# Routed experts: another order on GpSimd, down weights fetched once per expert, a copy added on ScalarE

## What is computed

```python
x = x + xattn(layernorm(x), ctx)                      # 16 sequences of 128 rows x 512
xt = layernorm(x).reshape(2048, 512)                  # 2048 tokens, h = 512
probs = softmax(xt @ Wr.T + bias)                     # 16 experts
w, idx = top_k(probs, 2); w = w / (w.sum() + 1e-9)
g, u = xt @ Wg[e], xt @ Wu[e]                         # 512 -> 256 each, expert e
y[e] = (silu(g) * u) @ Wd[e]                          # 256 -> 512
out = x + sum over the two chosen e of w * y[e] + shared expert(xt)
```

## Time and profile before

| | us |
|---|---|
| Median of 3 runs | 844.56 (840.42 to 849.78) |
| The profiled execution | 844.39 |
| Its span, first to last instruction | 842.6 |
| Mean granted PE clock, as a share of full speed | 0.917 |

### The profile page before, as it was taken

One profiled execution on the slowest core, in us unless ns is written; L12 is line 12 of the kernel. 1 busy time (PEld: TensorE's weight loads), 2 busy tenths in 40 slices (PEclk: granted clock), 3 DMA queues, 4 the chain that ended last, 5 costly groups with the idle time before them and its releaser, 6 DMA issues.

```text
span 842.6 us, 14106 instructions
## 1 busy us (share of the span) xinstructions
PE 689.8 (82%) x4136; PEld 334.9 (40%) x4136; DVE 400.5 (48%) x1426; ACT 315.2 (37%) x630; POOL 434.2 (52%) x640
## 2 busy tenths in 40 slices
PE   3378889999889888887699898959979887888791
PEld 1134445555555555433344444323323332333230
DVE  3387778888888887622425743212221222122210
ACT  3136556666666665552121122212222222222220
POOL 2466677777777777572000002246655454565542
PEclk9568899999999999898699999988998999999986
DMA  9967566566666664116777253567877777778772
GB/s 334 148 78 87 92 91 104 105 109 116 113 110 109 107 109 75 29 31 249 298 244 247 86 176 112 158 187 180 240 218 203 200 203 207 206 182 227 206 197 36
DMA packets 73684, 130.78 MB, mean 155 GB/s; under 512 B 18064, under 2 KB 42768, under 8 KB 71440
## 3 DMA queue, kind: packets, MB, share of 16 engines
q1 hardware_dynamic: 59264, 100.31, 47.7%
q0 software_dynamic: 9600, 20.98, 12.6%
q10 hardware_dynamic: 4752, 8.65, 3.1%
HBM read 84.55 MB, written 19.14 MB: 123 GB/s over the span
## 4 chain that ended last, share of the span: by engine, by line
DMA 31%; PE 28%; issue 13%; POOL 13%; DVE 5%; SPq 4%; ACT 3%; POOLq 2%; DVEq 0%; ACTq 0%
DMA out<-y_out,scatter_i 11%; DMA out<-y_out,scatter 10%; DMA wgu<-wgu 6%; PE bank L717 6%; POOL wgu L448 3%; POOL wgu L446 3%; PE bank L748 3%; PE bank L730 3%; SPq L322 3%; PE bank L556 3%; PE bank L572 2%; DMA rows<-xn_rows,gather_i 2%; PE bank L598 2%; PE bank L586 2%; POOL wgu L455 2%
## 5 line engine op out<-in xcount | busy, mean ns | idle before, releaser
L1081 DVE CUSTOM_DVE_ANT_0 bank<-bank,cb 128x192 f32<-128x192 f32 (+1 forms) x512 | 187.2, 415 | 60.4 <-PE bank L556 57.6
L730 PE MATMUL bank<-wgu,rowsT 128*64 x320 | 156.2, 634 | 2.7 <-DVE X L1308 2.3
L732 PE MATMUL bank<-X,rowsT 128*64 128x512 f32 x320 | 156.2, 634 | 0.0
L1294 DVE TENSOR_TENSOR act_in<-act_in,bank 128x256 f32<-128x256 f32 x56 | 23.6, 421 | 267.2 <-ACT act_in L979 259.1
L892 ACT ACTIVATE wgu<-bank 128x384 f32<-128x384 f32 (+1 forms) x256 | 125.2, 544 | 64.7 <-PE bank L572 64.1
L556 PE MATMUL bank<-wgu 96*128 96x192 bf16 (+1 forms) x512 | 97.4, 277 | 25.6 <-DMA wgu<-wgu 15.4
L495 POOL DMA_INDIRECT rows<-xn_rows,gather_i x40 | 47.7, 1193 | 125.9 <-issue 109.6
L446 POOL TENSOR_SCALAR_AFFINE_SELECT wgu<-wgu 128x512 f32<-128x512 f32 (+1 forms) x128 | 74.5, 582 | 71.1 <-ACT wgu L892 70.8
L509 POOL DMA_INDIRECT out<-y_out,scatter_i x40 | 60.3, 1508 | 84.1 <-DMA out<-y_out,scatter 43.5
L572 PE MATMUL bank<-wgu 99*128 99x192 bf16 (+1 forms) x512 | 73.7, 265 | 18.2 <-DMA wgu<-wgu 12.1
L509 POOL DMA_INDIRECT out<-y_out,scatter x40 | 58.3, 1456 | 52.6 <-DMA out<-y_out,scatter_i 30.0
(11 more groups left out here) (154 smaller groups left out, 938.0 us busy)
## 6 DMA issues: line engine op xcount, KB each, us to landing
X<-w_d SPq DMA_DIRECT2D x80, 512.0 KB
wgu<-wgu SPq DMA_DIRECT2D x192, 128.0 KB, 4.7
wgu<-w_gu SPq DMA_DIRECT2D x16, 1024.0 KB, 6.9
out<-y_out ACTq DMA_DIRECT2D x17, 256.0 KB, 6.0
wgu<-ctx SPq DMA_DIRECT2D x16, 256.0 KB, 4.5
xn_rows<-xn SPq DMA_DIRECT2D x16, 256.0 KB, 3.1
rows<-xn_rows ACTq DMA_DIRECT2D x16, 256.0 KB, 2.7
X<-x SPq DMA_DIRECT2D x1, 3072.0 KB, 16.0
```

Source lines behind the costliest of these rows:

```text
L730: mm(gb[k.buf][0:GROUP, :], rowsT[:, k.buf, c, 0:GROUP], wgu[:, bass.ds(e * 2048 + 512 * c, 512)], start=(c == 0), stop=(c == 3))
L732: last = mm(gb[k.buf][GROUP:P, :], rowsT[:, k.buf, c, GROUP:P], gu_half[:, k.buf, 512 * c:512 * c + 512], start=(c == 0), stop=(c == 3))
L1081: last = v.tensor_tensor_reduce(o, o, cb[:, B_MASK + off:B_MASK + off + w], 1.0, MASKED * 2.0, ALU.add, ALU.max, rowmaxes[n % 2][:, h + i, ...
```

## The change

It does five things in the routed stage.

1. **Adds.** `added` now counts by parity of the block, 32 for each block. Add (j, 0) waits for `result(j)` and, only if its expert is new, until both adds of block j-1 have landed. Add (j, 1) waits until both adds of block j-1 have landed, and for (j, 0) if its expert is new. Rows without a token are left out by the bounds check (`TOKENS - 1`, no error) and no longer written to the spare rows. The empty last slot now takes expert 15, as the other empty slots do, and slot 72 no longer counts as a new expert.
2. **Gathers.** `rows` has three buffers. POOL's order is gather(j+5), add_group(j, 0), add_group(j, 1).
3. **Down weights.** SP loads each expert's down weights once, 16 loads, into a ring of three in X (WD_RING), each when the last block of the expert three before is done (`last_i`), and one at a time.
4. **A copy on ACT.** Slot 0 reads the ring in place, at an address from a register. For slot 1, `wd_copy(k)`, last in ACT's step, reads two registers from tables, waits for down(k-1) and for the weights, and copies 128x1024 float32 inside X. `routed_down(k)` on PE waits for that copy.
5. **Tables.** `routing_blocks` also builds `place_i` (which ring buffer), `need_i` and `last_i`, and `order_i` in another form.

```diff
@@ load_wd is replaced, SP @@
+            for e in range(EXPERTS):
+                if e >= WD_RING:
+                    done = sp.value_load(last_i[0:1, e - WD_RING:e - WD_RING + 1], min_val=SEQS, max_val=SEQS + BLOCKS)
+                    stand(sp, SP, dn_mm, done)
+                sp.dma_start(wd[:, e % WD_RING * 1024:(e % WD_RING + 1) * 1024], w_d[e]).then_inc(wd_in, 16)
+                sp.wait_ge(wd_in, 16 * (e + 1))
@@ gather @@
-                n = SEQS + j
-                after(pool, t_mm, n - 1)
+                if j < 2:
+                    pool.wait_ge(t_mm, SEQS - 1 + j)
+                elif j > 2:
+                    pool.wait_ge(t_mm, SEQS + j - 2)
@@ add_group @@
-                if j > 0:
-                    pool.wait_ge(added[g], 16 * j)
-                if j > 0 or g > 0:
-                    stand(pool, POOL, added[1 - g], seen)
-                pool.wait_ge(y_ready, n + 1)
+                if g == 0:
+                    pool.wait_ge(y_ready, SEQS + j + 1)
+                    if j > 0:
+                        stand(pool, POOL, added[(j - 1) % 2], seen)
+                else:
+                    if j > 0:
+                        pool.wait_ge(added[(j - 1) % 2], 32 * ((j + 1) // 2))
+                    stand(pool, POOL, added[j % 2], seen)
...
-                    y_out[GROUP * g:GROUP * g + GROUP, n % 2, :], None, bounds_check=TOKENS + P - 1,
-                    oob_is_err=True, compute_op=ALU.add).then_inc(added[g], 16)
+                    y_out[GROUP * g:GROUP * g + GROUP, j % 2, :], None, bounds_check=TOKENS - 1,
+                    oob_is_err=False, compute_op=ALU.add).then_inc(added[j % 2], 16)
@@ POOL's loop @@
             for j in range(BLOCKS):
+                if j + AHEAD < BLOCKS:
+                    gather(j + AHEAD)
                 add_group(j, 0)
                 add_group(j, 1)
-                if j + AHEAD < BLOCKS:
-                    gather(j + AHEAD)
@@ PE @@
+            def wd_place(k):
+                return pe.value_load(place_i[0:1, (k.n - SEQS) * SUB:(k.n - SEQS) * SUB + 1], min_val=0,
+                                     max_val=WD_RING - 1)
...
-            def routed_down(k):
-                pe.wait_ge(wd_in[k.buf], 16 * SUB * (k.round - SEQS // 2 + 1))
+            def routed_down(k, place):
+                pe.wait_ge(wd_copied, k.n - SEQS + 1)
                 pe.wait_ge(at_ready, k.n + 1)
                 pe.wait_ge(y_ready, k.n - 1)
                 for c in range(2):
...
+                    mm(yb[k.buf][0:GROUP, :], actT[:, k.buf, c, 0:GROUP], wd[:, bass.ds(place * 1024 + 512 * c, 512)],
+                       start=(c == 0), stop=(c == 1))
+                    last = mm(yb[k.buf][GROUP:P, :], actT[:, k.buf, c, GROUP:P], wd_half[:, c, :],
+                              start=(c == 0), stop=(c == 1))
@@ result, ACT @@
-                    for g in range(2):
-                        act.wait_ge(added[g], 16 * (j - 1))
+                    act.wait_ge(added[j % 2], 32 * (j // 2))
@@ the end of ACT's step @@
                 if k.n + 2 < SEQS + BLOCKS:
                     rows_copy(k.plus(2))
+                wd_copy(k)
+
+            def wd_copy(k):
+                j = k.n - SEQS
+                place = act.value_load(place_i[0:1, j * SUB + 1:j * SUB + 2], min_val=0, max_val=WD_RING - 1)
+                need = act.value_load(need_i[0:1, j * SUB + 1:j * SUB + 2], min_val=16, max_val=16 * EXPERTS)
+                if j == 0:
+                    act.wait_ge(y_ready, SEQS // 2)
+                else:
+                    act.wait_ge(dn_mm, k.n)
+                stand(act, SCALAR, wd_in, need)
+                nc.scalar.copy(wd_half.rearrange("p a n -> p (a n)"),
+                               wd[:, bass.ds(place * 1024, 1024)]).then_inc(wd_copied, 1)
```

More of the change, by code:

```diff
@@ L49 @@
 RING = 4
+WD_RING = 3
 FIRST_UNIT, LAST_UNIT = -25, UNITS * (SEQS - 1) + 40
@@ L227, in xattn_moe_kernel @@
         rows_in = [sem(f"rows_in{i}") for i in range(2)]
-        wd_in = [sem(f"wd_in{i}") for i in range(2)]
+        wd_in, wd_copied = sem("wd_in"), sem("wd_copied")
         y_stored = [sem(f"y_stored{i}") for i in range(2)]
-        gathered = [sem(f"gathered{i}") for i in range(2)]
+        gathered = [sem(f"gathered{i}") for i in range(3)]
         added = [sem(f"added{i}") for i in range(2)]
@@ L704, in turn_rows @@
                 if shared:
-                    pe.wait_ge(rows_in[k.buf], 16 * (k.round + 1))
-                else:
-                    pe.wait_ge(gathered[k.buf], 16 * (k.round - SEQS // 2 + 1))
+                    held = k.buf
+                    pe.wait_ge(rows_in[held], 16 * (k.round + 1))
+                else:
+                    held = (k.n - SEQS) % 3
+                    pe.wait_ge(gathered[held], 16 * ((k.n - SEQS) // 3 + 1))
                 after(pe, t_ready, k.n - 1)
                 for c in range(4):
-                    last = nc.tensor.transpose(tb[k.buf][:, P * c:P * c + P], rows[:, k.buf, P * c:P * c + P], ident)
+                    last = nc.tensor.transpose(tb[k.buf][:, P * c:P * c + P], rows[:, held, P * c:P * c + P], ident)
                 last.then_inc(t_mm, 1)
@@ L755, in routed_down @@
                 for c in range(2):
-                    for j in range(SUB):
-                        part = slice(GROUP * j, GROUP * j + GROUP)
-                        last = mm(yb[k.buf][part, :], actT[:, k.buf, c, part], wd[:, k.buf, j, c, :],
-                                  start=(c == 0), stop=(c == 1))
+                    mm(yb[k.buf][0:GROUP, :], actT[:, k.buf, c, 0:GROUP], wd[:, bass.ds(place * 1024 + 512 * c, 512)],
+                       start=(c == 0), stop=(c == 1))
+                    last = mm(yb[k.buf][GROUP:P, :], actT[:, k.buf, c, GROUP:P], wd_half[:, c, :],
+                              start=(c == 0), stop=(c == 1))
                 last.then_inc(dn_mm, 1)
@@ L810, in routed_step @@
                 else:
-                    routed_down(k.plus(-1))
+                    routed_down(k.plus(-1), place)
+                place = wd_place(k)
                 if k.n + 1 < SEQS + BLOCKS:
@@ L816, in routed_step @@
                     turn_rows(k.plus(2), False)
-                return expert
+                return expert, place
             for k in range(1, 5):
@@ L1258, in routing_blocks @@
                 link(v.tensor_tensor(order[:, 1:BLOCKS * SUB], order[:, 1:BLOCKS * SUB],
-                                     expert_of[:, 0:BLOCKS * SUB - 1], ALU.add))
-                link(v.tensor_scalar(order[:], order[:], -1.0, 1.0, ALU.add, ALU.max))
+                                     expert_of[:, 0:BLOCKS * SUB - 1], ALU.mult))
+                link(v.tensor_scalar(order[:], order[:], 1.0, 1.0, ALU.add, ALU.max))
                 link(v.tensor_scalar(order_i[:], order[:], 16.0, None, ALU.mult))
```

61 lines of the change are left out of this document (33 added, 28 removed).

## The result

The changed kernel takes 782.63 us (median of 4 runs, 781.4 to 784.28). The kernel before, run beside it, takes 842.49 us (median of 4, 840.11 to 849.78). The difference of the medians is 59.9 us. The ratio is 0.9277, 95% interval 0.9214 to 0.9341: 7.2% faster. The forecast was 789 us with a range from 783 to 812. The direction and the bound (PE sets the pace) came out as forecast. The profiled execution of after took 781.99 us, with a span of 780.3 us, against 844.39 and 842.6 before.

A forecast was written before the change was run, and what follows sets the result against it. Late-landing adds were taken to bound the kernel, PE close behind. From 844.4 us: steps -55.5, tables +2.0, end -2.5, stalls +1, together -55, so 789 us, range 783 to 812.

The forecast's parts named there:

- PE sets the pace: Forecast case for the routed stage: PE's matmuls bound it, 6.11 to 6.25 us a step, 785 to 794 us; chance 0.60.
- the three waits: Routed stage: POOL waits 44.5 us for slot 1's adds, ACT 38.3 us for landings, PE 41.4 us for gathered rows.
- The step: SiLU to SiLU in the routed stage: 6.15 us instead of 7.61 over 38 steps, -55.5 us.
- Stalls at a change of expert: Routed stage: a few stalls where a load is met at a change of expert, +1 us.
- The end: Last block: last add sooner (2.6 us), (39, 0) freed (about 2), reads and copy exposed (2.3); taken as -2.5 us.
- The tables: Building the block tables: five more linked instructions on PE's path, 1.2 to 3.1 us, taken as +2.0 us.
- ACT's copy sticks out: Rival: ACT's copy or PE's sequencer adds 0.3 to 0.6 us a step, 800 to 812 us; chance 0.14.
- Adds stay slow: Rival: adds in flight and the gather crowd each other, an add takes 5 us again, 805 to 820 us; chance 0.13.
- The port: Rival: POOL slowed by DVE's copy becomes the bound, 6.5 us a block, 802 us; chance 0.04.
- Weights not the cause: Rival: little changes, the chain of adds keeps 7.2 us or more per block, 825 to 844 us; chance 0.04.
- Slower: Rival: adds with rows left out by the bounds check occupy POOL longer, above 844 us, up to 890; chance 0.04.
- an inner change: Expert changes inside a block: both adds take 9.7 us; PE not delayed, 1.9 us to spare at 4 us an add.

The follow-up runs named there:

- weights_only: The changed kernel with POOL's old order, waits, tables of the adds, two row buffers and spare-row writes put back; 799.6 us, ratio 0.9436 to before.
- pool_only: The changed kernel with the old 80 loads of down weights put back and no copy on ACT; 821.4 us, ratio 0.9707 to before.
- traffic_full: The changed kernel plus two loads of 512 KB per block into a buffer that nothing reads; 823.39 us, ratio 0.9786 to before.
- after_again: The changed kernel itself, unchanged, measured once more beside the kernel before; 783.81 us, ratio 0.9251.
- early_half: The changed kernel with slot 1's gate and up weights of block 17 placed in the shared expert's weight tile, for an earlier DVE copy; 783.14 us, ratio 0.9254.
- late_tables: The changed kernel with the building of the block tables cut in two and put between other shared-expert blocks; 779.7 us, ratio 0.9230 to before.
- copy_twice: The changed kernel with a second ACT copy of the same size, which nothing reads, ahead of the real one; 795.7 us, ratio 0.9449 to before.
- the gather in front: Old POOL waits with the new weights' part, the gather ahead of the adds and a third row buffer; 801.9 us, ratio 0.9481 to before.
- The two traffic kernels: The changed kernel plus one or two loads of 512 KB per block that nothing reads; 805.69 and 823.39 us, ratios 0.9590 and 0.9786.

## What the prediction had right, and which of its terms were wrong

**The mechanism was right in the main.** Late adds were one cause behind the three waits; weights_only and pool_only each take part of it off, and traffic_full brings it back by bytes alone. The price of an add, 3.7 to 4.3 us, was 3.98 in the mean. PE became the bound with a clock of 1.00. The copy and the sequencers are hidden. Of the cases, the one that held is "PE sets the pace". What failed is the size of terms in the sum. Of those that belong to the change, the allowance for register reads (0.04 us a step, nothing measured), the stalls (+1, none in this execution) and the end (-2.5, -4.4 measured) were each forecast too slow, some 5 us together, and the start, put at nothing without a reason, cost 1.9 more.

**The sum missed by 7 us, in five terms.** They are for the profiled executions, 844.39 and 781.99 us.

- *The step.* 6.15 forecast, 6.095 measured: 38 x 0.055 = 2.1 us. I had allowed 0.04 us for the register reads on PE and ACT. They cost nothing: PE is busy 200.00 of 200 us. The rest is mostly the last step, 5.67 us as before, which I had counted like the others.
- *Stalls at a change of expert.* +1 forecast, 0 in this execution. after_again has them: add (15, 1) waited 4.24 us for (15, 0), which met a load and landed after 4.95 us, landed itself after 5.5, and the step to block 19 took 8.81 us. early_half and late_tables have the same one. The term belongs in the range.
- *The end.* -2.5 forecast, -4.4 measured. The second add of the last block starts 771.54 - 769.84 = 1.70 us behind the first instead of 4.3, which is 2.6, as worked out. The exposed reads and copy, which were to cost 2.3 us, make PE wait 2.5, as the row of L761 shows. But PE had waited 0.89 us at this place before too, for the weights, so they cost 1.6 (timeline of before):

```profile
822.62 1.94 PE L758 MATMUL bank<-X,actT 128*64 128x512 f32 x8 [0.89 <-DMA X<-w_d]
```

  And add (39, 0) starts 0.88 us behind result(39) now, and 3.46 behind it before, when it waited for (38, 0): 2.6 us and not 2. So it starts 1.0 us earlier behind block 39's SiLU (8.07 against 9.07), where I had it 0.3 later. From the last add to the end it is 0.8 us less (8.76 against 9.53), since adds that write nothing land in 2.5 us. That I had called harmless and priced at nothing.
- *The start.* Nothing forecast, +1.9 measured. The first routed step took 10.21 us instead of 8.51, since its gate and up matmuls ran at half clock (granted clock 0.50 from 525.4 to 528.8 us, that is 1.2 GHz, where before it stays at 1.00, 2.4 GHz), behind the 2.33 us wait for DVE's copy that stood there before too (the timeline of after):

```profile
524.76 0.64 PE L731 MATMUL bank<-wgu,rowsT 128*64 x1 [2.33 <-DVE X L1343]
...
525.91 1.06 PE L731 MATMUL bank<-wgu,rowsT 128*64 x1
...
529.07 0.59 PE L731 MATMUL bank<-wgu,rowsT 128*64 x1
```

  A matmul takes 1.06 us there and 0.59 at full speed. In early_half, without the 2.33 us wait, the step from block 0 to 1 takes 6.11 us. Every profile with the weights' part and the copy in its old place shows it (10.1 to 10.2 us in all of them), before and pool_only don't (8.5). So it goes with the weights' part, though PE's wait is the same 2.33 us; by what way isn't settled.
- *The part that the change doesn't touch.* Nothing forecast, -4.0 measured. This is the largest miss, and it isn't one of the change: DVE enters `routing_blocks` at 457.70 us in after and at 461.74 in before. Its cause stays open (last section).

The tables came out right: 2.0 forecast, 1.9 measured (PE's wait grew from 3.90 to 5.79 us, timeline of after):

```profile
468.66 1.52 PE L794 MATMUL bank<-X 128*128 128x200 bf16 x8 [5.79 <-DVE X L1309]
```

The terms that belong to the change sum to 1.9 + 1.9 - 57.7 - 4.4 = -58.3 us, 3.3 us more than the -55 forecast, or 786 us. The other 4 us lie ahead of the change, within the spread of the executions there; that they are chance is likely, and isn't shown with one profile of before. So without luck in that part the time would have lain inside the range, and the terms of the change would still have been off by 3.3 us.

**Why the range was too short below.** Its lower end, 783, was built from terms of the change at their best, and the forecast was made against one profiled execution. The spread of the runs themselves had no place in it, although three runs of before lay 9.4 us apart. Upwards the rivals covered it, downwards nothing did. With the executions' own 4 us the end would have been 779. What the rows of before did not show are the adds that write nothing and the half clock at the start.

**The rivals.** *ACT's copy sticks out*: refuted, it has about 1 us of room, and copy_twice shows what it costs without (2.0%, of which the stalls at blocks 19 and 20 are some 0.7% that may have other causes). *Adds stay slow*: refuted for after; pool_only and traffic_full are what it would have looked like, at 821 and 823 us, dearer than the 805 to 820 that I gave it. *The port*: POOL's adds do grow beside DVE's copy (next section), and my reason against it was wrong: I had the adds 3.2 us behind the SiLU, when DVE is done; they come at 6.0 in the median, 37 of the 80 adds overlap a copy and 16 of these take 2.0 us or more. POOL has the room: 140.75 of 200 us busy. So the port was no bound, for another reason than mine. *Weights not the cause*: refuted by traffic_full. *Slower*: such an add occupies POOL for 1.40 us like any other.

**By hand through an inner change.** The forecast said that PE isn't held up at 4 us for an add and is late by 0.2 at 5. What was seen fits it: in after_again the two adds of block 15 took 4.95 and 5.5 us and PE stalled, in after no add of such a block held it up. But I had started from adds at 3.2 us. With adds at 6.0 the slack of 1.9 us isn't there at every block, so that no block stalled in after is partly luck of the loads' timing. One such stall of 2.7 us, with what follows it, is the difference between a step of 6.10 and of 6.19 in two executions of the same kernel. (the earlier trace rows gives the SiLUs at 646.04 and 652.15 to blocks 15 and 16. They are those of 16 and 17, and no number changes by it.)

## What to carry to other kernels

Where several engines wait for the same late thing, price that thing (here the landing of an add) and ask what shares its path; taking away one of the waits only moves it, as the gather in front did. Bytes that are loaded again and again cost time though no instruction waits for them, when another queue's small transfers are on the critical chain. Put the spread of the untouched part into the range of a forecast, on both sides.

## What the runs showed of the hardware

**Adds and bytes beside them.** A 64-row accumulating add of 2 KB rows lands in 3.98 us in the mean beside the 13 loads that are left in the stage, 4.7 with 0.5 MB and 5.45 with 1.0 MB more per block of 6 to 7 us. The queues of after from 560 to 760 us:

```profile
q0 software_dynamic: 7851, 15.72, 43.1%
q1 hardware_dynamic: 1728, 6.29, 10.4%
```

The indirect queue takes 43.1% of the engines' time for 15.72 MB, the plain one 10.4% for 6.29. Per byte the indirect transfers hold the engines 1.7 times as long. The Trainium skill, page DMA: Bandwidth & Descriptors, section Queues, rings and completion order, says that each DMA engine takes turns between the queues it has work for, a packet at a time; by it an add shares with a load instead of waiting for its end. The two traffic kernels agree with it, in that adds take longer the more bytes go beside them, but they don't show the packets taking turns.

**Adds of which every row is left out** land in 2.5 us: (38, 1) is issued at 766.76, and has landed at 769.25 by its semaphore. The row of the add at 769.84 names this landing as what it waited for. But that add starts 0.88 us behind the end of result(39) on ACT (768.96), as add (38, 0) did behind result(38) (764.18, 765.06), so it was ACT that released it. POOL is occupied for 1.40 us all the same.

**POOL beside DVE's copy.** The add at 610.13 took 2.09 us; DVE copied 128x2048 float32 at 610.71. DVE's timeline of after, that copy, one without an add beside it, and one inside an add that took 1.52 us (683.80):

```profile
604.61 1.23 DVE L1343 COPY X<-wgu 128x2048 f32 x1 [0.33 <-issue]
...
610.71 1.44 DVE L1343 COPY X<-wgu 128x2048 f32 x1 [0.33 <-issue]
...
683.99 1.23 DVE L1343 COPY X<-wgu 128x2048 f32 x1 [0.33 <-issue]
```

Of the 80 adds of after, the 43 that overlap no such copy took 1.39 to 1.49 us, and the 37 that do 1.43 to 2.45, the longest at 696.25. The copies took 1.22 to 1.44 us. So the two hinder each other by up to 1.0 us on POOL and 0.2 on DVE, and sometimes hardly at all: at 683.99 both ran at the same time and nearly at their usual lengths. By the rule of the Trainium skill that the prediction names (page SBUF — State Buffer, section Who interferes with whom), the two exclude each other for the whole instruction, so the copy at 683.99 should have waited for the add to end at 685.32. The trace doesn't agree: the copy ran at once and took 1.23 us, as at 604.61. Whether POOL's instruction needs the port only for a part of its time, no row shows.

**ACT's copy.** 128x1024 float32 from SBUF to SBUF took 1.045 us. The Trainium skill, page ScalarE: Activation LUTs, section What ACT_TABLE_LOAD costs, gives 186 ns + 0.833 ns per column for an ACTIVATE with immediate scale and bias. For 1024 columns that is an estimate of 1.04 us, and the trace agrees, though its instruction is a copy.

**The spread of what isn't touched.** In 14 profiled executions DVE entered `routing_blocks` between 455.5 and 463.4 us, all of them behind the same instructions on PE, ACT, DVE and POOL. The timelines of DVE, before and after, where `routing_blocks` begins:

```profile
461.74 1.47 DVE L1246 TENSOR_TENSOR X<-cf,count 128x1264 f32<-128x1264 f32 x1
```

```profile
457.70 1.47 DVE L1265 TENSOR_TENSOR X<-cf,count 128x1264 f32<-128x1264 f32 x1
```

What makes these 8 us was not looked into and stays open.
